# Second attention: half-height pairs for the low products, a third score bank, softmax sums in a bank of the maxima

## The reference, cut to what matters

```python
proj = jnp.einsum('bld,de->ble', x, W) + b          # 8 heads of 32
q, k, v = jnp.split(proj, 3, axis=3)
qk = jnp.einsum('bhqd,bhkd->bhqk', q, k)
emb_matrix = sinusoidal_embeddings(length, d_head)
indices = jnp.arange(length)[:, None] - jnp.arange(length) + length - 1
embeddings = emb_matrix[indices]
qe = jnp.einsum('bhqd,qkd->bhqk', q, embeddings)
weights = jax.nn.softmax((qk + qe) / jnp.sqrt(jnp.float32(d_head)), axis=-1)
output = jnp.einsum('bhqk,bhkd->bhqd', weights, v)
```

## Time and profile before

| | us |
|---|---|
| median of 3 runs | 2886.26 |
| lowest and highest | 2875.22, 2887.24 |
| the profiled execution | 2896.32 |
| its span, first to last instruction | 2894.5 |
| PE busy | 2541.5 (88%) |
| DVE busy | 2021.5 (70%) |
| POOL busy | 1971.0 (68%) |
| ACT busy | 1403.8 (48%) |
| mean granted TensorE clock | 0.937 |

### The profile page before, as it was taken

One profiled execution on the slowest core, in us unless ns is written; L12 is line 12 of the kernel. 1 busy time (PEld: TensorE's weight loads), 2 busy tenths in 40 slices (PEclk: granted clock), 3 DMA queues, 4 the chain that ended last, 5 costly groups with the idle time before them and its releaser, 6 DMA issues. The chain is left out here.

```text
span 2894.5 us, 47510 instructions
## 1 busy us (share of the span) xinstructions
PE 2541.5 (88%) x18598; PEld 867.1 (30%) x18598; DVE 2021.5 (70%) x3096; ACT 1403.8 (48%) x2558; POOL 1971.0 (68%) x767
## 2 busy tenths in 40 slices
PE   7899999999999999969889999999999999761265
PEld 2564222222222222235542222222222222240145
DVE  3475787787787877857876777777777777578144
ACT  4345555555555555523335555555555555440012
POOL 2123888888888888854447888878878878630763
PEclk8899999999999999989999999999999999875567
DMA  3994212222212312259764222233222232260337
GB/s 73 230 234 142 49 49 49 74 66 52 49 49 70 71 49 52 49 165 303 233 213 102 48 63 48 63 88 70 63 48 63 63 88 55 89 190 7 94 122 244
DMA packets 239568, 284.13 MB, mean 98 GB/s; under 512 B 65014, under 2 KB 172790, under 8 KB 236014
## 3 DMA queue, kind: packets, MB, share of 16 engines
q1 hardware_dynamic: 228848, 255.85, 33.0%
q0 software_dynamic: 6144, 16.85, 1.9%
q10 hardware_dynamic: 4352, 8.39, 0.8%
HBM read 171.32 MB, written 110.47 MB: 97 GB/s over the span
## 5 line engine op out<-in xcount | busy, mean ns | idle before, releaser
L849 POOL TENSOR_TENSOR room_af<-room_af 128x2048 f32<-128x2048 f32 x160 | 725.4, 4534 | 163.9 <-ACT room_af L821 149.7
L1197 POOL TENSOR_TENSOR bias<-bias 128x2048 f32<-128x2048 f32 x160 | 724.6, 4529 | 147.9 <-ACT bias L1169 134.0
L984 DVE TENSOR_REDUCE row_min_kf<-PS 128x1 f32<-128x1024 f32 x532 | 627.5, 1220 | 269.5 <-PE PS L976 268.0
L631 DVE CUSTOM_DVE_ANT_0 PS<-PS,bias 128x1024 f32<-128x1024 f32 x532 | 644.2, 1241 | 164.3 <-PE PS L619 147.6
L1169 ACT ACTIVATE bias<-PS 128x512 f32<-128x512 f32 x1024 | 557.2, 597 | 411.9 <-PE PS L1095 410.9
L821 ACT ACTIVATE room_af<-PS 128x512 f32<-128x512 f32 x1024 | 555.7, 595 | 397.3 <-PE PS L743 397.3
L1095 PE MATMUL PS<-stacks_kf 128*128 128x512 f16 x2048 | 532.9, 383 | 8.4 <-PEq L87 8.3
L736 PE MATMUL PS<-QS_af,KS_af 128*128 128x512 f16 x1024 | 333.8, 387 | 11.2 <-PEq L87 4.5
L1095 PEld LDWEIGHTS PS<-stacks_kf 128*128 128x128 f16 x2048 | 157.1, 97 | 448.8 <-ACT bias L1169 292.1
L769 PE MATMUL PS<-room_af,V_af 128*32 128x512 f32 x2048 | 272.8, 605 | 0.3 <-ACT room_af L821 0.3
L1115 PE MATMUL PS<-bias,V_kf 128*32 128x512 f32 x2048 | 272.7, 605 | 0.0
(11 more groups left out here) (183 smaller groups left out, 2874.8 us busy)
## 6 DMA issues: line engine op xcount, KB each, us to landing
stacks_kf<-query_key_halves SPq DMA_DIRECT2D x119, 256.0 KB, 7.3
query_key_halves<-bias SPq DMA_DIRECT2D x32, 768.0 KB, 4.3
query_key_halves<-room_af SPq DMA_DIRECT2D x32, 512.0 KB
KS_af<-query_key_halves SPq DMA_DIRECT2D x51, 256.0 KB, 4.7
QS_af<-query_key_halves SPq DMA_DIRECT2D x51, 256.0 KB, 6.9
V_kf<-values SPq DMA_DIRECT2D x9, 1024.0 KB, 10.7
V_af<-values SPq DMA_DIRECT2D x17, 512.0 KB, 8.8
stacks_kf<-query_key_halves SPq DMA_DIRECT2D x68, 128.0 KB, 9.4
```

Of the source, the lines that this page charges most:

```text
L631: nc.vector.tensor_tensor_reduce(out=max_ps[n % len(max_ps)], in0=max_ps[n % len(max_ps)], in1=bias_h[:, g * HG + j, z:z + N], scale=-1.0, ...
L849: nc.gpsimd.tensor_tensor(acc[:, u % 2], so_far, prob[:, n % PR], ALU.add).then_inc(acc_ok, 1)
L984: nc.vector.tensor_reduce(row_min[:, m:m + 1], max_ps[n % len(max_ps)], AX.X, ALU.min).then_inc(max_read, 1)
L1197: nc.gpsimd.tensor_tensor(acc[:, u % 2], so_far, prob[:, n % PR], ALU.add).then_inc(acc_ok, 1)
```

## The change

In the second attention:

1. The low products get 64 rows each. A new tile `lows` holds, for two heads, query low, turned query low and the maximum in 64 rows (heads 0 and 2 in rows 0 to 63, heads 1 and 3 in rows 64 to 127), and its counterpart of keys and embeddings. One row of the embedding is freed for the maximum: the slowest cosine is centred, its low half goes with a factor into one row together with the high half, and the turned query's last row is scaled. The zero rows of `stacks` and their fills go.
2. `scores` does two heads at a time: two full products into two banks, then the two 64-row products side by side.
3. There are three score banks. The output bank moves, and the bank of the sums is gone: the sums become one run of 12 products (tiles 6, 7 and `acc`) as one more job in the two banks of the maxima, in step DEN = 1 of the next unit. DVE copies them out (`take_sums`), which frees the bank, and takes reciprocals from the copy from step REC = 2. POOL finishes after step 5.
4. The order on PE in a step is now: scores 0 and 1, `weigh` of the step before, scores 2 and 3, maxima, and in step DEN the sums. TAKE stays 1.
5. A group load has 15 DMAs in place of 11, the embedding rows 20 in place of 10, and the set-up stores the embedding in 4 pieces in place of 2, with one operation more on DVE.

```diff
-                score_ps = [PS[:, 4 + i, :] for i in range(2)]
-                out_ps = PS[:, 6, :]
-                den_ps = PS[:, 7, :]
+                score_ps = [PS[:, 4 + i, :] for i in range(3)]
+                out_ps = PS[:, 7, :]
...
                     for j in range(HG):
-                        sp.dma_start(stacks[LEAD:LEAD + 1, slot, QL, j, first:first + CH].rearrange("p (t n) -> p t n", n=P),
+                        row = j % 2 * 2 * D + LAST
+                        sp.dma_start(lows[row:row + 1, slot, QL, j // 2, first:first + CH].rearrange("p (t n) -> p t n", n=P),
                                      max_row[j * TT:(j + 1) * TT, u % 2, :]).then_inc(m_in[u % 2], 16)
...
-                DEN, REC, TAKE, FIN = 2, 3, 1, 4
+                DEN, REC, TAKE, FIN = 1, 2, 1, 5
...
-                                if s >= 2:
-                                    pe.wait_ge(exps, s - 1)
-                                for n, (k_, q_) in enumerate(((KHL, QHH), (KH1, QL))):
-                                    last = nc.tensor.matmul(score_ps[s % 2], stacks[:, slot, k_, j, kt * P:(kt + 1) * P],
-                                                            stacks[:, slot, q_, j, first:first + CH], start=(n == 0), stop=(n == 1))
-                                last.then_inc(full, 1)
+                                for i in range(2):
+                                    if s + i >= 3:
+                                        pe.wait_ge(exps, s + i - 2)
+                                    nc.tensor.matmul(score_ps[(s + i) % 3], stacks[:, slot, KHL, j + i, kt * P:(kt + 1) * P],
+                                                     stacks[:, slot, QHH, j + i, first:first + CH], start=True, stop=False,
+                                                     skip_group_check=True)
+                                for i in range(2):
+                                    half = slice(2 * D * i, 2 * D * (i + 1))
+                                    nc.tensor.matmul(score_ps[(s + i) % 3], lows[half, slot, KH1, j // 2, kt * P:(kt + 1) * P],
+                                                     lows[half, slot, QL, j // 2, first:first + CH], start=False, stop=True,
+                                                     skip_group_check=True).then_inc(full, 1)
...
-                                if kt > ADDS:
-
-                                    if kt == ADDS + 1 and u >= 1:
-                                        pe.wait_ge(recd, PIECES * u)
+                                last.then_inc(weighed, 1)
+
+                            def denominators(n, u):
+                                pe.wait_ge(max_read, n - 1)
+                                pe.wait_ge(acc_ok, ADDS * (u + 1))
+                                parts = [prob[:, (KTU * u + kt) % PR] for kt in range(ADDS + 1, KTU)] + [acc[:, u % 2]]
+                                for i, part_ in enumerate(parts):
                                     for j in range(HG):
-                                        last = nc.tensor.matmul(den_ps[j * D:(j + 1) * D, :], den_w[:], prob[:, n % PR, j, :],
-                                                                start=(kt == ADDS + 1), stop=False, skip_group_check=True)
-                                last.then_inc(weighed, 1)
...
+                                        last = nc.tensor.matmul(max_ps[n % 2][j * D:(j + 1) * D, 0:CH], den_w[:], part_[:, j, :],
+                                                                start=(i == 0), stop=(i == len(parts) - 1),
+                                                                skip_group_check=True)
+                                last.then_inc(max_full, 1)
 
                             for n in range(NU * KTU + DEN + 1):
                                 if n < NU * KTU:
                                     scores(HG * n)
-                                    scores(HG * n + 1)
-                                    maxima(n)
-                                    scores(HG * n + 2)
-                                    scores(HG * n + 3)
                                 if 1 <= n <= NU * KTU:
                                     weigh(n - 1)
+                                if n < NU * KTU:
+                                    scores(HG * n + 2)
+                                    maxima(n)
                                 if n >= KTU and n % KTU == DEN:
-                                    denominators(n // KTU - 1)
+                                    denominators(job_at[(n // KTU - 1, "den")], n // KTU - 1)
...
+                            def take_sums(n, u):
+                                dve.wait_ge(max_full, n + 1)
                                 if u >= 2:
                                     dve.wait_ge(scaled, u - 1)
...
+                                nc.vector.tensor_copy(rec[:, u % 2, :], max_ps[n % 2][:, 0:CH]).then_inc(max_read, 1)
```

More of the change, by code:

```diff
@@ L368, in turned_high @@
                             act.wait_ge(added, u * G + g + 1)
-                            nc.scalar.copy(stg[:, u % 2, g, 2, :], rf[:, (u * G + g) % 2, :]).then_inc(r_high, 1)
+                            nc.scalar.activation(stg[:, u % 2, g, 2, :], rf[:, (u * G + g) % 2, :], ACT.Copy,
+                                                 scale=bcol[:, 2 * G:2 * G + 1]).then_inc(r_high, 1)
                         if kind == 0:
@@ L895, in tile @@
                     return es.enter_context(nc.sbuf_tensor(f"{name}_kf", shape, dt))
-                QHH, KHL, QL, KH1 = range(4)
-                LEAD = 2 * D
-                stacks = tile("stacks", [P, 2, 4, HG, N], F16)
+                QHH, KHL = range(2)
+                QL, KH1 = range(2)
+                LAST = 2 * D - 1
+                stacks = tile("stacks", [P, 2, 2, HG, N], F16)
+                lows = tile("lows", [P, 2, 2, HG // 2, N], F16)
                 V = tile("V", [P, 2, NT, C], F32)
@@ L939, in load_group @@
                     src = batch(qk_dram[1], b)[:, g].rearrange("a s (j d) n -> d (a s) j n", d=D)
-                    for r, st, s in ((0, QHH, 0), (1, QHH, 2), (2, QHH, 0), (3, QHH, 2), (0, QL, 1), (1, QL, 3), (0, KH1, 4)):
-                        sp.dma_start(stacks[r * D:(r + 1) * D, q % 2, st], src[:, s]).then_inc(stk[q % 2], 16)
+                    for r, s in ((0, 0), (1, 2), (2, 0)):
+                        sp.dma_start(stacks[r * D:(r + 1) * D, q % 2, QHH], src[:, s]).then_inc(stk[q % 2], 16)
+                    for first, s, rows in ((3 * D, 2, slice(0, D - 1)), (4 * D - 1, 3, slice(D - 1, D))):
+                        sp.dma_start(stacks[first:first + rows.stop - rows.start, q % 2, QHH], src[rows, s]).then_inc(stk[q % 2], 16)
+                    for h in range(2):
+                        for first, st, s, rows in ((0, QL, 1, D), (D, QL, 3, D - 1), (0, KH1, 4, D)):
+                            first += 2 * D * h
+                            sp.dma_start(lows[first:first + rows, q % 2, st], src[0:rows, s, h:HG:2]).then_inc(stk[q % 2], 16)
                     for r, c, s in ((0, 0, 4), (2, 0, 5), (0, 1, 5), (2, 1, 4)):
@@ L995, in attention_keys_first @@
                 job_at, jobs_done = {}, 0
-                for n in range(NU * KTU):
-                    for job in step_jobs[n]:
-                        job_at[job] = jobs_done
+                for n in range(NU * KTU + DEN + 1):
+                    if n < NU * KTU:
+                        for job in step_jobs[n]:
+                            job_at[job] = jobs_done
+                            jobs_done += 1
+                    if n >= KTU and n % KTU == DEN:
+                        job_at[(n // KTU - 1, "den")] = jobs_done
                         jobs_done += 1
@@ L1218, in _ @@
                                 u, piece = n // KTU - 1, n % KTU - REC
+                                if u >= 0 and n % KTU == DEN:
+                                    take_sums(job_at[(u, "den")], u)
                                 if u >= 0 and 0 <= piece < PIECES:
@@ L1287, in _ @@
                                      ).then_inc(x_in, 16)
-                    sp.wait_ge(e_low, 1)
-                    for s in range(2):
-                        sp.dma_start(edram[s * D:(s + 1) * D, :], e_p[:, s, :]).then_inc(e_out, 16)
+                    sp.wait_ge(e_low, 2)
+                    for row, (first_, last_), s in ((0, (0, D), 0), (D, (0, D - 1), 1), (2 * D - 1, (D, D + 1), 1),
+                                                    (2 * D, (D + 1, D + 2), 0)):
+                        sp.dma_start(edram[row:row + last_ - first_, :], e_p[first_:last_, s, :]).then_inc(e_out, 16)
                     sp.wait_ge(net_act, NETL)
@@ L1378, in _ @@
                                                                op1=ALU.subtract).then_inc(e_low, 1)
+                                dve.wait_ge(e_low, 1)
+                                nc.vector.scalar_tensor_tensor(out=e_p[D:D + 1, 1, :], in0=e_p[D:D + 1, 1, :], scalar=1.0 / SLOW,
```

(4 more changed lines are left out.)

76 lines of the change are left out of this document (38 added, 38 removed).

## The result

The changed kernel takes 3099.57 us (median; 3093.57 to 3101.91), the kernel before 2886.06 beside it: a ratio of 1.0746 [1.0716, 1.0776]. The forecast was 2933, with 2965 as the upper end. The sign was right and the size was not: +213 us against +47.

A forecast was written before the change was run, and what follows sets the result against it. PE was taken to bound the second attention; units of 32.24 us against 30.70 add 48 us over 31 units, the first unit -2.5, the stage +45, the token phase +2: +47, so 2933 us, range 2908 to 2965.

The forecast's parts named there:

- plain step with the bank's wait: Second attention: the second full product waits for the score bank ACT reads, so a step takes 3.28 us, not 3.16.
- step behind a delay: Second attention: a step following one with an extra delay behind its maxima, two per unit, stays at 3.16 us.
- W waits for the copy: Unit's second step: the products with V (W) wait for ACT's copy of the output bank, 1.84 us once a unit.
- the sums wait for the minimum: In their step, the softmax sums wait until DVE has read the first maxima tile: 1.16 us a unit.
- transposed maxima: Now last in their step on PE, they add 0.53 us a unit; their four small DMAs were taken to cost nothing.
- unit: Eight steps of the second attention (4 heads x 512 queries), 32 units in all: 32.24 us against 30.70 before.
- The copy out on DVE: DVE's copy of the sums lies under the next step's scores, before a product wants that bank: nothing.
- In the loop SP has time and the bytes are the same.: SP's 4 more DMAs per group load, near 0.6 us each, were taken to add nothing in the attention loop.
- the step put at +2 in the token phase: Token phase ahead of the second attention: issuing the additional DMAs could add 0 to 6 us, put at +2.
- Rival (c): Second attention: the clock falls at PE's holes, 15 to 30 us over half the units: 2948 to 2965 us; chance 0.15.
- Rival (d): Maxima DMAs land late, up to 1 us a unit (2965 us), or low pairs don't overlap (3040 us); chance 0.08.
- the two signs of being wrong: Second attention: the stage's clock row under 1.00, or a wait for a DMA at a unit's first score.

The follow-up runs named there:

- e2_split_take: e1_split with ACT's copy of the attended sums one step earlier, in the first step of the next unit (TAKE 0): 2888.38 us, ratio 0.9986.
- e5_mid: e2_split_take with the sums placed between the two maxima of their step, on PE and on DVE: 2843.01 us, ratio 0.987.
- e1_split: The changed kernel with each 31-row DMA (group loads and embedding tables) issued as 16 and 15 rows: 2969.12 us, ratio 1.0277.
- e3_all3: e2_split_take with the sums ahead of both maxima of their step, on PE and on DVE: 2876.55 us, ratio 0.9943.
- e8_serial: e2_split_take with both low products of a pair in the same 64 rows, unable to run side by side (wrong result): 2963.3 us, ratio 1.0286.
- e4_before31: The kernel before with two of the 11 DMAs of each group load cut into 31 rows and 1 row: 3069.59 us, ratio 1.0606.
- e9_cover: e1_split with the maxima ahead of the products with V in each unit's second step, copy not moved: 2881.14 us, ratio 1.0008.

## Why the prediction was right in sign and wrong in size

**What held.** The terms of the loop, each as the prediction put it and as an undisturbed unit showed it:

| term, us | forecast | measured |
|---|---|---|
| plain step with the bank's wait | 3.28 | 3.25 |
| step behind a delay | 3.16 | 3.15 |
| W waits for the copy | 1.84, 31 times | 1.78, 31 times |
| the sums wait for the minimum | 1.16 | 1.10 |
| sums in one run | 2.71 | 2.71 (1649.06 to 1651.77) |
| transposed maxima | 0.53 | 0.54 (3.79 less 3.25) |
| unit | 32.24 | 32.05 |

The bank's wait of 0.12 us a step, read from the first attention, was 0.10. Removing one wait after the other gave each its price back: the copy 1.80 (e2_split_take), the sums 1.07 (e5_mid). The maxima landed in time, or nearly: PE's products waited for them 1.0 us in all, in e1_split 2.2. The copy out on DVE cost nothing in the change's own order, as I had said; it has a price as soon as the sums come ahead of the maxima (e3_all3). The low pairs overlap (e8_serial). So the sign was no luck: with its 31-row DMAs cut in two (e1_split) the change still makes the kernel 2.8% slower.

**What failed: "In the loop SP has time and the bytes are the same."** I priced the new DMAs by their number, near 0.6 us each, and by their bytes. Those prices are right, as e1_split shows: with 28 DMAs for the tables and 18 for a group, more than the change has itself, SP issues them at about 0.5 us each, and the token phase is no longer than before. The price lay in the shape. A DMA of 31 rows runs on one engine, by its share of 0.07, at 25 GB/s, and the next DMA in SP's queue stands behind it (5.08 us in the load shown). The step put at nothing in the loop made the seventh steps 77 us longer, 75.7 of them PE's wait, and the steps behind some 20 more, at a low clock (the eighth steps are 23 us over, and in e1_split some 3); the step put at +2 in the token phase (0 to 6) cost 54. With the cut into 16 and 15 rows it is 135 us less, and the change of shape done to the kernel before, 31 rows and 1, costs that one 6%, 175 us. Nothing in the rows of before shows a DMA with such a row count, and the prediction should have said so: this was an operation that the trace does not show, and I priced it by the nearest rows and gave it no bound on the other side. Of the first group in the token phase PE waited 3.1 us already; it now waits 20.0.

**Rival (c) came true beside the forecast, not in place of it.** The clock fell in the second step of 13 of 31 units of the changed kernel (22 us) and of 18 of e1_split (30 us); I had given 15 to 30 us for half of the units. I treated it as one case among others, with 0.15. Its reason was partly wrong: I had taken two holes close together for the danger, and the clock fell behind the first, of 1.7 to 1.8 us, before the second began. With the 31 rows cut the time is 76 us above before: 42 for the units, less 2.5, 30 for the clock, and some 6 left over, of which the traces put 3 in the experts. That lies at 2962, in the upper part of this rival (2948 to 2965). The forecast of +47 alone would have needed the clock to stay up.

**Rival (d)** looked for a DMA that lands late, and had the wrong one: the small ones with the maxima cost PE 1.0 us in all, the group load 75.7. Of the two signs of being wrong that the prediction named, the first showed as it was put (the clock row of the stage is 0.94) and the second mostly in another place: the long waits for a DMA stand at the first maxima of a group, and those at the first score of a unit are 1.0 us in all.

**The experts, and what is not settled.** The experts behind the attention, which none of these kernels changes, took 394.7 us in the trace of the kernel before and 384.3 in that of the changed one (from the last product with V to the end). The other traces show that this goes with where and when a kernel ran, and not with the kernel: the four that ran together on one chip (e1_split, e2_split_take, e3_all3, e4_before31) have 395 to 398, the six on two other chips 382 to 385, and the kernel before, measured beside them, took 2892.77 us in the first case, 2882.83 and 2879.96 in the others. The trace of before is of an execution of 2896.32, ten above its median, which is also why the traces differ by 203 us and the medians by 213. So times of different groups of runs are compared by their ratios. Why the chips differ in this phase is open, and so is what makes the clock fall in one unit and not in the next.

## What to carry to other kernels

Before a tile's rows are cut to make room for one row, look at how many rows each piece leaves: 31 + 1 costs what 16 + 15 + 1 does not, 135 us here. When products are halved and a group of them becomes shorter, every wait that lay under it comes out; list what each later instruction of that engine needs and when it is there, and move the releasing work (here ACT's copy, and the place of the sums) together with it. The halved products, with the rows cut otherwise and these two moved, make the kernel 1.3% faster (e5_mid, 2843.01 us); without that they made it 7.5% slower.

## What the runs showed of the hardware

- While the DMAs of 31 rows were under way the DMA share was 0.07 and the rate 25 GB/s, where loads of 32 rows ran at 0.95 and 196 GB/s; and SP stood 12 to 17 us at four to six DMAs with 31-row ones among them, at the DMA behind each (0.28 us for 31 rows, 5.08 for the next). With 17 rows among them eight DMAs took SP 8.7 us; with 16 and 15, 3.7.
- A clock that in e1_split was otherwise at 1.00 through the loop (its first 6 us apart) fell to 0.50, for 3.4 or 6.8 us at a time, within 1.2 us of PE's resuming from a hole of 1.7 to 1.8 us, in 13 to 20 units of 31 in four kernels. One hole of 1.1 us a unit (e2_split_take) never did it, nor did one of 0.7 (e9_cover).
- A long wait is paid twice: behind the DMA waits of up to 10 us the clock fell too, and in 13 of 16 cases the next step ran 4.0 to 5.3 us instead of 3.15.
